# Query and recurrence products of a vision tower as sums of f16 halves, on one core

## Chip, core and metric

One core of a Trainium2 chip runs the whole program. The metric is the device time of one execution in microseconds (us); the time of the kernel before is the median of three. Engines are named as in the profile: PE is TensorE (PEld its weight loads), DVE is VectorE, ACT is ScalarE, POOL is GpSimd, SP is SyncE, which only issues DMAs.

## The reference, cut to what matters

```python
x = features.reshape(b, c, h, s, w, s)                 # 32 x 256 x 16 x 4 x 16 x 4
reduce_feats = x.mean((3, 5)).reshape(b, c, hw).transpose(0, 2, 1)
q = _ln(reduce_feats, ln_q_w, ln_q_b) @ Wq.T           # the queries
kv = _ln(unf, ln_kv_w, ln_kv_b) @ Wkv.T
attn = softmax(einsum('bhpd,bhpnd->bhpn', q * scale, k)); aggre = einsum('bhpn,bhpnd->bhpd', attn, v)
h = reduce_feats + aggre @ proj_w.T + proj_b           # then a class token in front of each image
...
xp = einsum('tbi,hi->tbh', layernorm(h), W_ih) + b_ih + b_hh
h_new = tanh(xp_t + h @ W_hh.T)                        # scan over the 32 images, 257 tokens wide
h = h + hiddens
h = h + moe(layernorm(h))                              # 8 experts, the best 2 of each token
```

All of it is f32; the recurrence runs over the images, one step per image for all its tokens.

## The kernel before, in words

The program has two stages. Stage A makes tokens, attention, recurrence and routing; stage B is the experts. Only stage A is touched. It works in 64 units of 128 tokens (two units an image), one slot per unit, and a slot carries four units at different depths: `u` (front) is loaded, averaged and given its queries; `v = u-1` (mid) gets scores and softmax; `w = u-2` (back) gets values and output projection; `z = u-3` (end) gets its step of the recurrence; `u-4` (late) is routed. Each engine has a function `slot` whose calls stand in a fixed order, written by hand; engines meet only at semaphores (`wait(engine, semaphore, ...)`). An engine carries out its queue in order, so a wait holds up all that stands behind it.

The steps that matter, in the order of a slot:

- PE `means` (L876) averages the pixels; ACT `mean_out` brings the mean from the bank FB to `rT`; DVE `mean_stats` and `mean_norm` make the norm `rn`; PE `turn_rn` (L884) transposes it into FB; ACT `rn_out` (L725) copies it to `rnT`; PE `queries` (L892) multiplies it with `wq_s` into FB; ACT `q_out` adds the bias and writes `qT`; PE `project` (L904) goes on with it.
- DVE `unmask` (L1151) cuts the scores `sm` out of the bank SB, PE `fold_patches` (L935) sums them, DVE `logits_in`, `total`, `divide` (up to `pr`, L1175) with ACT `exps` between make the softmax, PE `turn_p` (L942) transposes it.
- For the recurrence DVE `token_norm` (L1206) makes `xn`, PE `turn_xn` (L993) transposes it into the bank RB, ACT `xn_out` copies it to `xnT`, PE `recur` (L1005 with `hh_s` and the old `hT`, L1007 with `ih_s` and `xnT`) makes the new state, ACT `hidden` applies tanh into `hT`, PE `turn_h` turns it back, DVE `token_out` adds it to the tokens.
- POOL makes the inverse roots; of them `rs_wide` is what `turn_rs` (L912), the last PE step of a slot, waits for. SP reloads the buffers `xc` and `xp` as steps free them.

In some slots DVE also does a piece of the routing at the end of its list (`route_piece`: six steps or so in most of the eight pieces of a group of tiles). Ahead of the slots stands a prologue that scales the weights: DVE makes `wq_s` (L1267), then `rn` of unit 0, then `wk_s` (from L1270); the last link before the slots on PE is the class token's `xnT` (ACT L858).

Of the kernel before, what the change touches and what calls it, by code (L numbers as in the profile page):

```python
# [5 lines left out]
P = 128  # L6
# [10 lines left out]
CC = C // P  # L17
# [99 lines left out]
def vit_tower(nc, xc_in, xp_in, cls_tok, ln_q_w, ln_q_b, wqT, ln_kv_w, ln_kv_w_col, ln_kv_b, wk, wvT, projT, proj_b,  # L117
# [6 lines left out]
    with ctx:  # L124
# [50 lines left out]
        def sa(name, shape, dt=F32):  # L175
# [11 lines left out]
        wq_s = sa("wq_s", [P, CC, C])  # L187
# [3 lines left out]
        ih_s = sa("ih_s", [P, CC, C])  # L191
        hh_s = sa("hh_s", [P, CC, C])
# [10 lines left out]
        rnT = sa("rnT", [P, CC, P])  # L203
# [25 lines left out]
        xnT = sa("xnT", [P, CC, P + 1])  # L229
        hT = [sa(f"hT{i}", [P, CC, P + 1]) for i in range(2)]  # L230
# [9 lines left out]
            rT_ps rT_done q_stat q_var q_ve_done q_rs_done rn_done rc_done rn_ps rnT_done q_ps qT_done u_ps u_done  # L240
            st_done px_ve_done px_done wide_done own_done rep_ps rep_done s_ps s_masked c_ps sc_done c_max c_sub ex_done
            p_sum p_rec p_done pt_ps pd_done z_ps z_done zt_ps zT_done a_ps aT_done pj_ps h_done h_stat h_var h_ve_done h_rs_done
            xn_done nt_ps xnT_done h_ps hT_done ht_ps h2_done clsH_done
# [21 lines left out]
        stage_b = xc[1][:, :, :].rearrange("p c (h n) -> p (c h) n", n=C)  # L265
        projb_row = stage_b[:, 0, :]
# [270 lines left out]
        def _(sp):  # L537
            row_of = lambda a, n: a.partition_broadcast(n)
            for dst, src in ((spread[:, :], spread_in), (ident[:, :], ident_in)):
# [5 lines left out]
                     (ih_s[:, :, :], wihT.rearrange("(c p) n -> p c n", p=P)),  # L545
                     (hh_s[:, :, :], whhT.rearrange("(c p) n -> p c n", p=P)),
# [9 lines left out]
            sp.wait_ge(s["w_ready"], 2)  # L556
            load_xc(sp, 1, 1)
# [65 lines left out]
        def _(pool):  # L623
# [4 lines left out]
            for i in range(2):  # L628
                pool.memset(hT[i][:, :, :], 0.0).then_inc(s["mem_set"], 1)
            pool.memset(ones[:, :], 1.0).then_inc(s["mem_set"], 1)  # L630
            pool.wait_ge(s["mem_set"], 5)
# [33 lines left out]
            def keep_cls(pool, z):  # L665

                wait(pool, s["hT_done"], z, 2, 2)
                b = z.j * HALVES + z.k // HALVES
                pool.tensor_copy(clsH[:, :, bass.ds(b, 1)], hT[0][:, :, P:P + 1]).then_inc(s["clsH_done"], 1)
# [31 lines left out]
        def _(act):  # L701
# [20 lines left out]
            def rn_out(act, u):  # L722

                wait(act, s["rn_ps"], u, 1, 1)
                act.activation(rnT[:, :, :].rearrange("p c t -> p (c t)"), FB[:, 0:C], ACT.Copy).then_inc(s["rnT_done"], 1)  # L725

            def q_out(act, u):

                wait(act, s["q_ps"], u, 1, 1)
                for m in range(CC):  # L730
                    act.activation(qT[:, m, :], FB[:, m * P:(m + 1) * P], ACT.Identity, bias=qb_col[:, m:m + 1]).then_inc(s["qT_done"], 1)
# [41 lines left out]
            def xn_out(act, z):  # L773

                wait(act, s["nt_ps"], z, 1, 1)
                wait(act, s["h_ps"], z, 1, 0)
                act.activation(xnT[:, :, 0:P], RB[:, 0:C].rearrange("p (c t) -> p c t", t=P), ACT.Copy).then_inc(s["xnT_done"], 1)

            def hidden(act, z):

                wait(act, s["h_ps"], z, 1, 1)
                n = P + 1 if z.two == 0 else P
                if z.two == 0 and z.k > 0:
                    act.wait_ge(s["clsH_done"], z.k // HALVES)
                for m in range(CC):
                    act.activation(hT[z.two][:, m, 0:n], RB[:, m * 256:m * 256 + n], ACT.Tanh,
                                   bias=rnn_b[:, m:m + 1]).then_inc(s["hT_done"], 1)
# [13 lines left out]
            def slot(act, u, front, mid, back, end, late):  # L801
# [26 lines left out]
                if late:  # L828
                    route_logits(act, u.k - 4, FB)
                if mid:  # L830
                    z_out(act, v, [0, 1])
# [25 lines left out]
            act.wait_ge(s["mem_set"], 5)  # L857
            act.activation(xnT[:, :, P:P + 1], FB[:, 0:CC * B].rearrange("p (c b) -> p c b", b=B)[:, :, 0:1],  # L858
                           ACT.Copy).then_inc(s["w_ready"], 1)
            act.wait_ge(s["prep_act"], 4)  # L860
# [3 lines left out]
        def _(pe):  # L864
# [22 lines left out]
            def queries(pe, u):  # L887

                wait(pe, s["rnT_done"], u, 1, 1)
                for m in range(CC):  # L890
                    for c in range(CC):
                        last = mm(FB[:, m * P:(m + 1) * P], wq_s[:, c, m * P:(m + 1) * P], rnT[:, c, :],  # L892
                                  start=(c == 0), stop=(c == CC - 1))
                last.then_inc(s["q_ps"], 1)
# [101 lines left out]
            def recur(pe, z, m):  # L996

                n = P + 1 if z.two == 0 else P
                o = RB[:, m * 256:m * 256 + n]
                w = slice(m * P, (m + 1) * P)  # L1000
                if m == 0:
                    wait(pe, s["xnT_done"], z, 1, 1)
                    wait(pe, s["hT_done"], z, 2, -2)
                for c in range(CC):
                    mm(o, hh_s[:, c, w], hT[z.two][:, c, 0:n], start=(c == 0), stop=False)  # L1005
                for c in range(CC):
                    last = mm(o, ih_s[:, c, w], xnT[:, c, 0:n], start=False, stop=(c == CC - 1))  # L1007
                if m == CC - 1:
                    last.then_inc(s["h_ps"], 1)

            def turn_h(pe, z):

                wait(pe, s["hT_done"], z, 2, 2)
                for c in range(CC):
                    last = pe.transpose(RB[:, c * P:(c + 1) * P], hT[z.two][:, c, 0:P], ident[:, :])
                last.then_inc(s["ht_ps"], 1)

            def slot(pe, u, front, mid, back, end, late):
# [16 lines left out]
                if mid:  # L1035
                    fold_patches(pe, v)
                if end:
                    turn_xn(pe, z)
                if front:
                    queries(pe, u)  # L1040
# [42 lines left out]
            pe.wait_ge(s["prep_dve"], 4)  # L1083
            queries(pe, first)
            pe.wait_ge(s["mem_set"], 5)
# [3 lines left out]
            pe.wait_ge(s["prep_dve"], 8)  # L1089
# [3 lines left out]
            pe.wait_ge(s["prep_dve"], 10)  # L1093
# [8 lines left out]
            pe.wait_ge(s["w_ready"], 2)  # L1102
            pe.wait_ge(s["tri_done"], 1)
# [4 lines left out]
        def _(dve):  # L1108
# [33 lines left out]
            def mean_norm(dve, u):  # L1142
# [3 lines left out]
                dve.tensor_scalar(rn[:, :], rT[:, :], qmv[:, 0:1], q_rs[:, 0:1], ALU.subtract, ALU.mult).then_inc(s["rn_done"], 1)  # L1146

# [60 lines left out]

            def token_out(dve, z):
# [14 lines left out]
            def slot(dve, u, front, mid, back, end, late):  # L1224
# [8 lines left out]
                if mid:  # L1233
                    unmask(dve, v)
                if end:
                    token_norm(dve, z)
# [8 lines left out]
                if mid:  # L1245
                    total(dve, v)
                    divide(dve, v)
                if front:
# [6 lines left out]
                if end:  # L1255
                    token_out(dve, z)
                for g, part in pieces_now(u.k):
# [35 lines left out]
            dve.tensor_tensor(cvec[:, :], RB[:, 0:C], projb_row, ALU.add).then_inc(s["w_ready"], 1)  # L1293
            over_slots(dve, slot)
# [359 lines left out]
```

## Time and profile before

| | |
|---|---|
| median of 3 runs | 1449.83 us (1447.99 to 1450.88) |
| the profiled execution | 1449.13 us, its span 1447.3 us |
| PE busy | 1312.8 us (91%) |
| DVE busy | 1029.4 us (71%) |
| ACT busy | 816.7 us (56%) |
| POOL busy | 713.2 us (49%) |
| mean granted TensorE clock | 0.974 |
| DMA, mean | 293 GB/s |

Busy time is a mean over both stages. Stage A runs from the start to about 1100 us, its slots begin at 31 us; stage B fills the rest. An f32 product appears as two records on PE (and two weight loads), so `queries`, four products in the code, are eight records; an f16 product is one.

### The profile page before, as it was taken

Reading aid. Unit: us, or ns where it says so; the run is one execution under the profiler, and the core shown is the slowest. Engines: PE = TensorE matmul, PEld = TensorE weight load, DVE = VectorE, ACT = ScalarE, POOL = GpSimd, SP = SyncE. Lnnn points to the kernel's source line nnn. Section 1 sums busy time; section 2 is a strip of 40 time slices with the busy share of each in tenths; the row PEclk is TensorE's granted clock in tenths of the full one; section 3 lists DMA queues with packets and bytes.
Section 4 is the critical chain, followed back from the end, with each engine's and each line's share of the span. In section 5 each row is a group of like instructions: output and inputs, shape, how many; then the busy total and the mean of one; then the engine's idle time right before and its main releaser. Section 6 shows DMA issues by size and latency. Waiting matters only on the chain. (4 is left out here: it accounts for less than half of the span.)

```text
span 1447.3 us, 61906 instructions
## 1 busy us (share of the span) xinstructions
PE 1312.8 (91%) x25169; PEld 1071.8 (74%) x25169; DVE 1029.4 (71%) x2724; ACT 816.7 (56%) x1999; POOL 713.2 (49%) x852
## 2 busy tenths in 40 slices
PE   5799999999999999999999999999986999899960
PEld 3577788778777787777777777777865999777850
DVE  4677777777767777787876676778764686588874
ACT  1466556555656556555555555556555777555630
POOL 1344344434443434343466666664421577776476
PEclk8999999999999999999999999999998999999995
DMA  8999889999999999988899999998543788799897
GB/s 270 406 320 320 294 299 309 314 299 303 303 296 307 301 302 314 303 288 275 295 335 323 334 342 344 336 333 301 187 131 112 229 293 292 251 316 337 284 289 220
DMA packets 186614, 423.70 MB, mean 293 GB/s; under 512 B 23968, under 2 KB 89312, under 8 KB 186208
## 3 DMA queue, kind: packets, MB, share of 16 engines
q1 hardware_dynamic: 170336, 380.27, 77.3%
q0 software_dynamic: 14048, 38.16, 8.2%
q8 instruction: 205, 3.36, 0.9%
q10 hardware_dynamic: 1952, 1.32, 0.3%
q14 instruction: 73, 0.60, 0.1%
HBM read 332.26 MB, written 87.39 MB: 290 GB/s over the span
## 5 line engine op out<-in xcount | busy, mean ns | idle before, releaser
L1123 DVE BATCH_NORM_STATS2 st<-xp 128x6 f32<-128x512 f32 x512 | 340.3, 696 | 15.7 <-DMA xp<-xpix 15.2
L651 POOL TENSOR_TENSOR rs_px<-px_ve,half_neg 128x16 f32<-128x16 f32 x64 | 187.0, 2922 | 175.6 <-DVE px_ve L1128 175.6
L765 ACT ACTIVATE zT<-bank 128x512 f32<-128x512 f32 x256 | 138.6, 597 | 82.1 <-PE bank L966 82.1
L758 ACT ACTIVATE z_s<-bank 128x512 f32<-128x512 f32 x256 | 138.7, 597 | 80.7 <-PE bank L956 80.7
L925 PE MATMUL bank<-xc,u 128*32 128x64 f32 x8192 | 147.3, 220 | 25.1 <-issue 24.4
L925 PEld LDWEIGHTS bank<-xc,u 128*32 128x32 f32 x8192 | 130.1, 110 | 51.2 <-issue 40.3
L739 ACT ACTIVATE u<-bank 128x512 f32<-128x512 f32 x256 | 132.2, 602 | 49.1 <-PE bank L904 49.1
L1420 POOL DMA_INDIRECT y<-ys_dram,slot x130 | 129.3, 995 | 59.0 <-issue 36.3
L636 POOL TENSOR_TENSOR q_rs<-q_ve,half_neg 128x1 f32<-128x1 f32 x64 | 35.1, 549 | 244.5 <-DVE q_ve L1140 244.5
L966 PE MATMUL bank<-ident,z_s 128*128 128x128 f32 x1024 | 150.7, 280 | 2.2 <-issue 1.4
L412 POOL DMA_INDIRECT xs_dram<-xrow,slot x130 | 130.8, 1006 | 39.5 <-issue 34.6
L876 PE MATMUL bank<-xp,spread 128*32 128x256 f32 x2048 | 126.8, 389 | 14.5 <-DMA xp<-xpix 13.3
L956 PE MATMUL bank<-xp,pd 64*32 64x256 f32 x4096 | 126.7, 382 | 3.2 <-ACT u L739 3.2
L1457 ACT ACTIVATE g<-bank,b_s 128x256 f32<-128x256 f32 x172 | 82.0, 477 | 75.8 <-PE bank L1507 54.2
L966 PEld LDWEIGHTS bank<-ident,z_s 128*128 128x128 f32 x1024 | 112.0, 141 | 14.5 <-issue 1.6
L1192 DVE TENSOR_TENSOR h_s<-bank,rc 128x256 f32<-128x256 f32 x64 | 27.2, 425 | 125.1 <-PE bank L985 125.1
L1520 PE MATMUL bank<-xp,gh 128*128 x344 | 94.2, 274 | 14.3 <-DVE gl L1554 14.0
L876 PEld LDWEIGHTS bank<-xp,spread 128*32 128x32 f32 x2048 | 61.6, 111 | 56.4 <-issue 17.6
L1570 DVE SCALAR_TENSOR_TENSOR y_s<-bank,b_rep 128x512 f32<-128x512 f32 x86 | 59.4, 690 | 58.2 <-PE bank L1522 40.7
L956 PEld LDWEIGHTS bank<-xp,pd 64*32 64x32 f32 x4096 | 74.6, 107 | 34.7 <-issue 11.6
L1135 DVE BATCH_NORM_STATS2 qst<-rT 128x6 f32<-128x256 f32 x64 | 27.3, 426 | 96.0 <-ACT rT L720 95.9
L1505 PE MATMUL bank<-xT,xp 128*128 128x256 f16 x344 | 94.7, 275 | 0.3 <-ACT gh L1457 0.3
(178 smaller groups left out, 3142.6 us busy)
## 6 DMA issues: line engine op xcount, KB each, us to landing
xp<-xpix SPq DMA_DIRECT2D x256, 512.0 KB
xc<-xg SPq DMA_DIRECT2D x256, 512.0 KB
xc<-xs_dram SPq DMA_DIRECT2D x86, 256.0 KB
ys_dram<-y_s SPq DMA_DIRECT2D x86, 256.0 KB
xs_dram<-zero SPq DMA_DIRECT2D x57, 384.0 KB, 5.6
base_dram<-h SPq DMA_DIRECT2D x65, 128.0 KB, 5.7
rows_dram<-tok SPq DMA_DIRECT2D x65, 128.0 KB
hb<-base_dram SPq DMA_DIRECT2D x65, 128.0 KB, 4.3
```

The costliest lines, as they stand in the source:

```text
L412: pool.indirect_dma_start(xs_dram[g], bass.IndirectOffsetOnAxis(ap=slot_u[k][0:n, t:t + 1], axis=0), xrow[i][0:n, :], None).then_inc(sent[ ...
L651: pool.tensor_tensor(rs_px[:, :], px_ve[:, :], half_neg[:, :], ALU.pow).then_inc(s["px_done"], 1)
L739: act.activation(uv[:, k, :, :, :], BIG[k][:, :].rearrange("p (m a t) -> p m a t", m=CC, t=TS), ACT.Copy).then_inc(s["u_done"], 1)
L758: act.activation(z_s[:, r, 2 * half:2 * half + 2, :].rearrange("p a c -> p (a c)"), BIG[2 * r + half][:, :], ACT.Copy).then_inc(s["z_done" ...
L765: act.activation(zT[:, c, :, :].rearrange("p h (a r t) -> p r h a t", r=2, t=TS)[:, r, :, :, :], BIG[f][:, :].rearrange("p (a h t) -> p h ...
L876: last = mm(FB[32 * k:32 * k + 32, 0:C], spread[:, 24 - 8 * q:56 - 8 * q], xp[u.x][:, 4 * k + q, :], start=(q == 0), stop=(q == 3))
L925: last = mm(SB[32 * k:32 * k + 32, (2 * n + r) * SUB:(2 * n + r + 1) * SUB], u_s[u.two][:, c, g, :, :].rearrange("p h t -> p (h t)"), xc[u ...
L956: last = mm(BIG[2 * r + half][32 * k:32 * k + 32, n * C:(n + 1) * C], pd[64 * r:64 * r + 64, g, :, :].rearrange("p h t -> p (h t)"), xp[v. ...
L966: last = pe.transpose(BIG[f][:, n * P:(n + 1) * P], z_s[:, r, n, c * P:(c + 1) * P], ident[:, :])
L1123: dve.bn_stats(st[:, j, :], xp[u.x][:, 2 * j:2 * j + 2, :].rearrange("p i c -> p c i")).then_inc(s["st_done"], 1)
L1420: pool.indirect_dma_start(y[q][0:n, :], None, ys_dram[g], bass.IndirectOffsetOnAxis(ap=slot_u[k][0:n, t:t + 1], axis=0)).then_inc(ga_in[q] ...
L1505: mm(o, wh, xh, start=(c == 0), stop=False)
```

## The change

The two products for the queries and the recurrence are no longer f32 products. Each f32 operand is split into an f16 high half and an f16 low half (the rest), and each product is three f16 products added up in the bank: high with high, low weight with high, high weight with low. So `queries` has 12 f16 products for 4 f32 ones, `recur` 24 for 8. Weights are scaled by 64 before they are split; ACT takes the factor out again (`scale=1.0 / WSC`).

High halves are written by ACT in the copies that were there (`rnT_h`, `xnT_h`), and for the state by a new copy `hidden_high` behind the routing logits. Low halves are three new DVE steps: `mean_low` behind `unmask`, `token_low` behind `divide`, `hidden_low` behind `token_out`. `queries` waits for `mean_low`, `recur` for `token_low` and for the `hidden_low` of the slot before. On PE `queries` now stands ahead of `turn_xn`. The state `hT` in f32 has one buffer for two.

In the prologue DVE splits the query weights (two steps over 128x512 before `rn`) and does `mean_low` for unit 0; ACT and DVE split the recurrence weights (two steps each) behind the class token's `xnT_h`, and PE and SP wait for that (`rec_w`) before the slots and before the loads of `xc` 1 and `xp` 2.

```diff
 def rn_out(act, u):
     wait(act, s["rn_ps"], u, 1, 1)
-    act.activation(rnT[...], FB[:, 0:C], ACT.Copy).then_inc(s["rnT_done"], 1)
+    wait(act, s["q_ps"], u, 1, 0)
+    wait(act, s["rnl_done"], u, 1, 0)
+    act.activation(rnT_h[...], FB[:, 0:C], ACT.Copy).then_inc(s["rnT_done"], 1)
...
+def hidden_high(act, z):
+    n = P + 1 if z.two == 0 else P
+    wait(act, s["hT_done"], z, 2, 2)
+    act.activation(hT_h[z.two][:, :, 0:n], hT[:, :, 0:n], ACT.Copy).then_inc(s["hh_done"], 1)
...
 def queries(pe, u):
     wait(pe, s["rnT_done"], u, 1, 1)
+    wait(pe, s["rnl_done"], u, 1, 1)
...
-            last = mm(FB[...], wq_s[...], rnT[:, c, :], ...)
+            mm(o, wq_h[:, c, w], rnT_h[:, c, :], start=(c == 0), stop=False)
+            mm(o, wq_l[:, c, w], rnT_h[:, c, :], start=False, stop=False)
+            last = mm(o, wq_h[:, c, w], rnT_l[:, c, :], start=False, stop=(c == CC - 1))
...
 def recur(pe, z, m):
         wait(pe, s["xnT_done"], z, 1, 1)
-        wait(pe, s["hT_done"], z, 2, -2)
+        wait(pe, s["xnl_done"], z, 1, 1)
+        wait(pe, s["hl_done"], z, 1, -1)
...
+def mean_low(dve, u):
+    wait(dve, s["rnT_done"], u, 1, 1)
+    wait(dve, s["q_ps"], u, 1, 0)
+    dve.tensor_tensor(rnT_l[:, :, :], FB[...], rnT_h[:, :, :], ALU.subtract).then_inc(s["rnl_done"], 1)
...
+def token_low(dve, z):
+    wait(dve, s["xnT_done"], z, 1, 1)
+    dve.tensor_tensor(xnT_l[:, :, 0:P], RB[...], xnT_h[:, :, 0:P], ALU.subtract).then_inc(s["xnl_done"], 1)
+
+def hidden_low(dve, z):
+    wait(dve, s["hh_done"], z, 1, 1)
+    dve.tensor_tensor(hT_l[z.two][:, :, 0:n], hT[:, :, 0:n], hT_h[z.two][:, :, 0:n], ALU.subtract)...
...
+dve.wait_ge(s["prep_pe"], 1)
-    chain(dve.tensor_scalar(wq_s[:, c, :], raw_q[:, c, :], lq_w[:, c:c + 1], None, ALU.mult))
+    chain(dve.tensor_scalar(raw_q[:, c, :], raw_q[:, c, :], lq_w[:, c:c + 1], None, ALU.mult))
+chain(dve.tensor_scalar(wq_h[:, :, :], raw_q, WSC, None, ALU.mult))
+chain(dve.scalar_tensor_tensor(wq_l[:, :, :], raw_q, WSC, wq_h[:, :, :], ALU.mult, ALU.subtract))
 mean_norm(dve, first)
+mean_low(dve, first)
...
+for raw, high in ((raw_ih, ih_h), (raw_hh, hh_h)):
+    act.activation(high[:, :, :], raw, ACT.Copy, scale=WSC).then_inc(s["rec_hi"], 1)
...
+dve.wait_ge(s["rec_hi"], 2)
+for raw, high, low in ((raw_ih, ih_h, ih_l), (raw_hh, hh_h, hh_l)):
+    dve.scalar_tensor_tensor(low[:, :, :], raw, WSC, high[:, :, :], ALU.mult, ALU.subtract)...
```

On PE, in the middle of a full slot, this is the order before, from the last turn of `z_s` to `values` (`ident,xn` is `turn_xn`, `rnT,wq_s` are the queries):

```order
L966 MATMUL bank<-ident,z_s 128x128 x4
L935 MATMUL bank<-sm,pick 32x128 x4
L993 MATMUL bank<-ident,xn 128x128 x2
L892 MATMUL bank<-rnT,wq_s 128x128 x4
L977 MATMUL bank<-zT,wv_s 32x128 x16
```

And this is the same place of the change; the three products of the queries come four times.

```order
L989 MATMUL bank<-ident,z_s 128x128 x4
L958 MATMUL bank<-sm,pick 32x128 x4
L914 MATMUL bank<-rnT_h,wq_h 128x128
L915 MATMUL bank<-rnT_h,wq_l 128x128
L916 MATMUL bank<-rnT_l,wq_h 128x128
...
L1016 MATMUL bank<-ident,xn 128x128 x2
L1000 MATMUL bank<-zT,wv_s 32x128 x16
```

The turn of `xn` has moved from ahead of the queries to behind them, so nothing stands between `fold_patches` and the queries.

On DVE, from `unmask` to `pd` of a full slot, the order before is:

```order
L1151 TENSOR_TENSOR sm<-bank,fold 128x512
L1206 TENSOR_SCALAR xn<-h_s,hmv,h_rs 128x256
L313 TENSOR_SCALAR tok<-h_1,emv,ers 128x256
L1123 BN_STATS st<-xp 128x6
...
L1173 RECIPROCAL rden<-den 128x8
L1175 TENSOR_TENSOR pr<-ex,rden 128x128
L1123 BN_STATS st<-xp 128x6
L1128 TENSOR_SCALAR px_ve<-st 128x16
L1183 TENSOR_TENSOR pd<-bank,rs_own 128x512
```

In the change two steps have come in, `rnT_l` (`mean_low`) and `xnT_l` (`token_low`):

```order
L1187 TENSOR_TENSOR sm<-bank,fold 128x512
L1181 TENSOR_TENSOR rnT_l<-bank,rnT_h 128x256
L1242 TENSOR_SCALAR xn<-h_s,hmv,h_rs 128x256
L316 TENSOR_SCALAR tok<-h_1,emv,ers 128x256
L1152 BN_STATS st<-xp 128x6
...
L1209 RECIPROCAL rden<-den 128x8
L1211 TENSOR_TENSOR pr<-ex,rden 128x128
L1248 TENSOR_TENSOR xnT_l<-bank,xnT_h 128x2x128
L1152 BN_STATS st<-xp 128x6
L1157 TENSOR_SCALAR px_ve<-st 128x16
L1219 TENSOR_TENSOR pd<-bank,rs_own 128x512
```

Everything from `xn` to `pr` now stands behind one new step, and what follows `pr` behind two.

## Rows read from the trace of the kernel before

**Rows 1.** By stretch: busy us of PE, PEld, DVE, ACT, POOL; clock; DMA share; GB/s.

```profile
200.00:300.00 100.00, 98.42 (x2205) 79.64 (x2202) 74.31 (x215) 59.79 (x152) 40.92 (x52) 1.00 0.91 306
```

**Rows 2.** Timeline, PE in one slot: start us, us, engine, line, records [idle before].

```profile
224.91 0.33 PE L912 MATMUL bank<-ident,rs_wide 128*128 128x128 f32 x1
...
231.43 0.43 PE L935 MATMUL bank<-sm,pick 128*32 128x128 f32 x8
...
231.78 0.44 PE L993 MATMUL bank<-ident,xn 128*128 128x128 f32 x2
...
232.06 1.06 PE L892 MATMUL bank<-rnT,wq_s 128*128 128x128 f32 x8
...
235.54 0.61 PE L1005 MATMUL bank<-hT,hh_s 128*128 128x129 f32 x4
...
237.33 1.03 PE L985 MATMUL bank<-pj_s,aT 128*128 128x256 f32 x4
...
240.79 0.33 PE L912 MATMUL bank<-ident,rs_wide 128*128 128x128 f32 x1
```

**Rows 3.** Timeline, the same slot on DVE, ACT and POOL.

```profile
227.66 0.43 DVE L1135 BATCH_NORM_STATS2 qst<-rT 128x6 f32<-128x256 f32 x1 [1.67 <-ACT rT L720]
...
230.69 0.68 DVE L1151 TENSOR_TENSOR sm<-bank,fold 128x512 f32<-128x512 f32 x1
...
230.90 0.39 ACT L725 ACTIVATE rnT<-bank 128x256 f32<-128x256 f32 x1 [1.19 <-PE bank L884]
...
231.29 0.41 DVE L1206 TENSOR_SCALAR xn<-h_s,hmv,h_rs 128x256 f32<-128x256 f32 x1
...
234.57 0.29 DVE L1175 TENSOR_TENSOR pr<-ex,rden 128x128 f32<-128x128 f32 x1
...
238.76 0.41 POOL L654 TENSOR_TENSOR rs_wide<-rs_px,ones 128x128 f32<-128x128 f32 x1
```

**Rows 4.** Timeline, f16 products of the routing ranks, PE, then PEld.

```profile
660.76 0.37 PE L440 MATMUL bank<-oh,ones 128*128 128x128 f16 x4
...
660.81 0.39 PE L440 MATMUL bank<-oh,ones 128*128 128x120 f16 x5
...
660.87 0.15 PEld L440 LDWEIGHTS bank<-oh,ones 128*128 128x128 f16 x2
```

**Rows 5.** Groups by line on DVE: busy us, mean ns | idle before, releasers.

```profile
L1559 DVE TENSOR_TENSOR xT<-bank,xT 128x512 f16<-128x512 f32 x86 | 58.8, 684 | 3.5 <-ACT xT L1442 3.4
...
L1192 DVE TENSOR_TENSOR h_s<-bank,rc 128x256 f32<-128x256 f32 x64 | 27.2, 425 | 125.1 <-PE bank L985 125.1
```

**Rows 6.** Waits of the whole span: us in total, times, longest.

```profile
PE bank L925 <- issue: 24.4, 27, 2.1
```

**Rows 7.** Timeline of one slot with such a stall.

```profile
424.98 0.41 DVE L1206 TENSOR_SCALAR xn<-h_s,hmv,h_rs 128x256 f32<-128x256 f32 x1
425.14 0.38 ACT L725 ACTIVATE rnT<-bank 128x256 f32<-128x256 f32 x1 [1.19 <-PE bank L884]
...
428.05 0.29 DVE L1168 TENSOR_REDUCE den<-ex 128x8 f32<-128x128 f32 x1 [0.28 <-ACT ex L751]
```

**Rows 8.** Timeline, PE in a slot behind a routing piece.

```profile
618.88 0.42 PE L935 MATMUL bank<-sm,pick 128*32 128x128 f32 x8 [0.47 <-DVE sm L1151]
```

**Rows 9.** Timeline of the prologue.

```profile
18.82 0.35 DVE L1267 TENSOR_SCALAR wq_s<-xc,lq_w 128x256 f32<-128x256 f32 x1 [0.59 <-DMA pj_s<-projT]
18.84 1.05 PE L1074 MATMUL bank<-lq_b,xc 128*128 128x1 f32 x8 [1.92 <-DMA pj_s<-projT]
...
20.70 0.68 DVE L1270 TENSOR_TENSOR xc<-xc 128x512 f32<-128x512 f32 x1
...
21.62 0.38 ACT L725 ACTIVATE rnT<-bank 128x256 f32<-128x256 f32 x1 [0.29 <-PE bank L884]
...
31.32 3.24 PE L876 MATMUL bank<-xp,spread 128*32 128x256 f32 x32 [0.31 <-ACT xnT L858]
```

**Rows 10.** Groups by line, an f16 copy on ACT: columns as in Rows 5.

```profile
L799 ACT ACTIVATE xp<-xc 128x512 f16<-128x512 f32 x16 | 8.7, 632 | 2.1 <-DMA xc<-w 2.1
```

More of the change, by code:

```diff
@@ L186, in vit_tower @@
         qb_col = sa("qb_col", [P, CC])
-        wq_s = sa("wq_s", [P, CC, C])
+        wq_h, wq_l = [sa(f"wq_{n}", [P, CC, C], F16) for n in "hl"]
         wk_s = sa("wk_s", [P, CC, C])
@@ L190, in vit_tower @@
         pj_s = sa("pj_s", [P, CC, C])
-        ih_s = sa("ih_s", [P, CC, C])
-        hh_s = sa("hh_s", [P, CC, C])
+        ih_h, ih_l = [sa(f"ih_{n}", [P, CC, C], F16) for n in "hl"]
+        hh_h, hh_l = [sa(f"hh_{n}", [P, CC, C], F16) for n in "hl"]
         cvec = sa("cvec", [P, C])
@@ L202, in vit_tower @@
         rn = sa("rn", [P, C])
-        rnT = sa("rnT", [P, CC, P])
+        rnT_h, rnT_l = [sa(f"rnT_{n}", [P, CC, P], F16) for n in "hl"]
         qT = sa("qT", [P, CC, P])
@@ L228, in vit_tower @@
         xn = sa("xn", [P, C])
-        xnT = sa("xnT", [P, CC, P + 1])
-        hT = [sa(f"hT{i}", [P, CC, P + 1]) for i in range(2)]
+        xnT_h, xnT_l = [sa(f"xnT_{n}", [P, CC, P + 1], F16) for n in "hl"]
+        hT = sa("hT", [P, CC, P + 1])
+        hT_h = [sa(f"hT_h{i}", [P, CC, P + 1], F16) for i in range(2)]
+        hT_l = [sa(f"hT_l{i}", [P, CC, P + 1], F16) for i in range(2)]
         zero = sa("zero", [P, C])
@@ L556, in _ @@
             sp.wait_ge(s["w_ready"], 2)
+            sp.wait_ge(s["rec_w"], 3)
             load_xc(sp, 1, 1)
@@ L829, in slot @@
                     route_logits(act, u.k - 4, FB)
+                if end:
+                    hidden_high(act, z)
                 if mid:
@@ L1036, in slot @@
                     fold_patches(pe, v)
+                if front:
+                    queries(pe, u)
                 if end:
                     turn_xn(pe, z)
-                if front:
-                    queries(pe, u)
                 if back:
@@ L1102, in _ @@
             pe.wait_ge(s["w_ready"], 2)
+            pe.wait_ge(s["rec_w"], 3)
             pe.wait_ge(s["tri_done"], 1)
@@ L1207, in token_norm @@
                                   ALU.mult).then_inc(s["xn_done"], 1)
+            def token_low(dve, z):
+                wait(dve, s["xnT_done"], z, 1, 1)
+                dve.tensor_tensor(xnT_l[:, :, 0:P], RB[:, 0:C].rearrange("p (c t) -> p c t", t=P), xnT_h[:, :, 0:P],
+                                  ALU.subtract).then_inc(s["xnl_done"], 1)
+            def hidden_low(dve, z):
+                n = P + 1 if z.two == 0 else P
+                wait(dve, s["hh_done"], z, 1, 1)
+                dve.tensor_tensor(hT_l[z.two][:, :, 0:n], hT[:, :, 0:n], hT_h[z.two][:, :, 0:n],
+                                  ALU.subtract).then_inc(s["hl_done"], 1)
             def token_out(dve, z):
@@ L1234, in slot @@
                     unmask(dve, v)
+                if front:
+                    mean_low(dve, u)
                 if end:
@@ L1247, in slot @@
                     divide(dve, v)
+                if end:
+                    token_low(dve, z)
                 if front:
@@ L1256, in slot @@
                     token_out(dve, z)
+                    hidden_low(dve, z)
                 for g, part in pieces_now(u.k):
@@ L1293, in _ @@
             dve.tensor_tensor(cvec[:, :], RB[:, 0:C], projb_row, ALU.add).then_inc(s["w_ready"], 1)
+            dve.wait_ge(s["rec_hi"], 2)
+            for raw, high, low in ((raw_ih, ih_h, ih_l), (raw_hh, hh_h, hh_l)):
+                dve.scalar_tensor_tensor(low[:, :, :], raw, WSC, high[:, :, :], ALU.mult, ALU.subtract).then_inc(s["rec_w"], 1)
+            dve.wait_ge(s["w_ready"], 2)
+            dve.tensor_tensor(xnT_l[:, :, P:P + 1], FB[:, 0:CC * B].rearrange("p (c b) -> p c b", b=B)[:, :, 0:1],
+                              xnT_h[:, :, P:P + 1], ALU.subtract).then_inc(s["rec_w"], 1)
             over_slots(dve, slot)
```

60 lines of the change are left out of this document (35 added, 25 removed).

## The prediction

> **What bounds the kernel now.** First the busy time by stretch: in a stretch from the middle of stage A, PE works 98.42 of 100 us at the full granted clock (1.00), the upper of its two levels, DVE 74.31, ACT 59.79, POOL 40.92 [rows 1]. So PE bounds the slots, and a slot is as long as PE's list. The timeline of one slot shows it: from one turn of `rs_wide` to the next 15.88 us (224.91 to 240.79) without an idle note on PE [rows 2]. The question is who is late next when PE's list gets shorter, and that is read from the same slot on DVE [rows 3]: it idles 1.67 us ahead of `qst`, and from there its steps follow each other without a gap to `pr`, which ends at 234.86, only 0.68 us before PE starts the recurrence at 235.54. The new steps go into just this chain. Not all slots look so: in 27 of 63 PE stands inside the scores (L925) for something that the profile doesn't show, 24.4 us in all [rows 6], and behind a routing piece it waits for DVE's `sm` (0.47 us in the one shown) [rows 8]; I put 8 slots down to that, somewhat fewer than the long pieces of two groups, since the second group's steps are shorter. That leaves 28 plain slots.
>
> **The products.** The recurrence's 16 f32 records take 237.33 - 235.54 = 1.79 us, 0.112 each [rows 2]. The trace has f16 products of 128 columns, each with a weight load: the one of 128 columns starts at 660.76, the next at 660.81, so 0.05 apart, and their two weight loads lie within 0.15 us, overlapping [rows 4]. Half an f32 record is 0.056; I take that. Recurrence: 24 x 0.056 = 1.34, a gain of 0.45 us. Queries: 8 x 0.112 = 0.90 to 12 x 0.056 = 0.67, a gain of 0.23. On PE's list alone that is 0.68 us a slot.
>
> **mean_low.** It subtracts f16 from a PSUM bank, 128x256. DVE's nearest row of that size is `h_s` with 0.425 us; half as wide is `pr` with 0.29, twice as wide and with f16 written is L1559 with 0.684 [rows 3, 5]. I take 0.42, between 0.29 and 0.68. It stands behind `unmask`, which leaves DVE free at 231.29, and needs `rnT`, which ACT ends at 231.29 [rows 3]: with 0.08 for the signal it runs from 231.37 to 231.79. PE takes a DVE result 0.06 us after its end (`sm` ends at 231.37, L935 starts at 231.43) [rows 2, 3], so the queries start at 231.85. `fold_patches` is done at 231.78 and `turn_xn` no longer fills the gap: PE waits 0.07 us. Turning `xn` behind the queries costs nothing, since `xn` is ready long before 232.5. Queued behind `mean_low` on DVE are `xn`, the routing norm, two statistics and the whole softmax. `xn` starts at 231.71 in place of 231.29, and `pr`, with no gap between to take it up, ends at 234.86 + 0.42 = 235.28.
>
> **token_low.** The same price. Steps overlap by 0.08 us (`xn` starts at 231.29, `sm` ends at 231.37), so it runs from 235.20 to 235.62, and the recurrence starts at 235.68, 0.14 later than before. The 0.23 us of the queries are thus lost in waits for DVE; with 1.34 us the recurrence ends at 237.02, 0.31 before the old 237.33. **A plain slot gains 0.31 us**, 28 of them 8.7. What else moves there has cover: `rs_wide` shifts by 0.42 + 0.34 to end at 239.93, while PE wants it at 240.48; without that cover each further tenth on DVE would cost a tenth.
>
> **hidden_high, hidden_low.** One ACT copy (at most 0.63, L799, which is twice as wide [rows 10]) and one DVE step (0.42). ACT is 60% busy [rows 1]; the DVE step lies in the 1.67 us ahead of `qst` [rows 3], and its result is wanted a slot later. Nothing; without DVE's cover, 0.34 us a slot, as behind the routing pieces.
>
> **Stalled slots.** Where PE stalls in the scores, `rnT` is late: in the slot shown it ends at 425.52, when DVE has been free since 424.98 [rows 7]. Before, DVE went on with `xn`; now it stands. `xn` starts at 425.94, 0.96 late. Some comes back, as `den` had waited 0.28 us there for the exponentials [rows 7], which now come no later than DVE's own steps allow: I take 0.6 at `pr`. In a plain slot 0.42 at `pr` became 0.14 at the recurrence, 0.28 less, so here the recurrence starts 0.6 - 0.28 = 0.32 later and a slot gains 0.45 - 0.32 = 0.13. Bounds: a gain of 0.31 if all is taken up, a loss of 0.2 if nothing is. 27 x 0.13 = 3.5.
>
> **Slots behind a routing piece.** There DVE is late already [rows 8], `hidden_low` adds its 0.34 and the recurrence moves by about what it gains: 0, between +0.2 and -0.3 each. Sum of the slots: 8.7 + 3.5 = 12.2 us.
>
> **The prologue** [rows 9, 10]. (a) The weights are now scaled in place, so DVE waits until PE has read them: 19.89 in place of 18.82, 1.1. (b) Two steps of 128x512 ahead of `rn`, 0.68 each: 1.4. (c) `mean_low` of unit 0 makes DVE wait for `rnT`: L1270 would start at 22.0 + 0.08 + 0.34 = 22.4, not 20.70: 1.7. From L1270 a chain of DVE, POOL and PE leads to `xnT`, on which PE waits until 31.32, so all 4.2 us arrive there. (d) Behind it come two ACT copies (0.63 and 0.52 with their overlap), two DVE steps (0.69 and 0.61) and a tiny one, less the 0.3 that PE's wait took before: about 2.5, which `rec_w` puts ahead of PE's first slot and of SP's loads behind it (`xc` 1 to `xp` 3, which move with the slot that needs them). 6.7 us, once; between 5 and 8, as (c) or (d) may hide a little. No later slack gives it back while slots follow each other on PE.
>
> **Sum.** 12.2 - 6.7 = 5.5 us. The profiled execution took 1449.13 us, 0.7 under the median of the runs and inside their spread: 1443.6 from the one, 1444.3 from the other. Forecast **1444**.
>
> **A rule against the change.** On pace, the row says 0.05 us from one f16 product of 128 columns to the next with loads in between [rows 4], though all these loads bring the same tile. The Trainium skill, "TensorE: Matmul & The Clock Gate", section "Back-to-back issue gap", says that a sustained stream of weight load and matmul goes at about 81 ns for 128 columns. By that the recurrence would take 24 x 0.081 = 1.94 us, longer than now, and the time an estimated 1472 us. The trace doesn't agree; the sum goes by the row.
>
> **The rivals.** *PE's gain arrives whole*: DVE takes the low halves up somewhere (cheap subtractions, near 0.29, and `rnT` earlier). Against it stands DVE's chain without a gap. 55 x 0.68 - 6.7 gives 1418. Chance 0.08.
> *DVE's chain gets longer than priced* (slower): the low halves write and read f16 beside a bank, and a row of that kind is L1559 with 0.684 us [rows 5]. At that price the recurrence starts 0.14 + 0.52 later and a slot loses 0.21: 55 x 0.21 + 6.7 gives 1467. It decides from 6.7 / 55 = 0.12 us gain per slot, that is once the two steps together come 0.19 us later than I put them; halfway it gives 1455. For it: nothing on DVE is slack there, and `rnT` is just in time. Chance 0.21.
> *The f16 products are paced by their weight loads*, 0.10 us each alone [rows 4], since here every product has weights of its own, so the change doesn't do what it says: 24 x 0.10 = 2.4, 0.75 more a slot, 1497. Against it: the overlap in the rows. Chance 0.05.
> *The prologue hides* behind loads that the slots wait for: 1439. Chance 0.05. My forecast has 0.61, its own range is 1437 to 1451.
>
> **How the numbers follow.** A measurement of this kernel tells 0.2%, 2.9 us, from no change. Of the forecast's 0.61, 0.45 lies below 1446.9, 0.13 within, 0.03 above; of the slower rival 0.05 lies within. Faster 0.45 + 0.08 + 0.05 = 0.58, same 0.18, slower 0.24. The range leaves out the whole gain, the weight loads and the far end of the slower rival: 1434 to 1458.
>
> **What the profile after would show.** Plain slots of 15.57 us; the f16 records 0.056 apart; on PE waits for `rnT_l` (under 0.1 us) and for `xnT_l` ahead of the recurrence (about 0.2) in plain slots; DVE idle ahead of `rnT_l` in stalled ones; the first slot starting near 38 us. Wrong, if plain slots are near 15.2 (no chain on DVE), above 15.76 (the low halves cost more), or if the records lie 0.08 or more apart.

## The result and the profile after

The change makes the kernel slower: 1487.82 us median (1485.09 to 1490.09) beside 1450.36 of before, a ratio of 1.0224 with a 95% interval of 1.0179 to 1.0269; that it is slower is clear, whether by 2% is not. The forecast was 1444.0 with a range up to 1458. The profiled execution took 1490.09 us, 0.15% over the median.

First a plain slot, one in which PE idles nowhere. The timeline of PE in after answers to [rows 2], with the two new DVE steps beside it; it goes from one turn of `rs_wide` to the next, and in the columns are start, length, line, tiles and count:

```profile
207.38 0.33 PE L935 MATMUL bank<-ident,rs_wide 128*128 128x128 f32 x1
...
213.78 0.42 DVE L1181 TENSOR_TENSOR rnT_l<-bank,rnT_h 128x256 f16<-128x256 f32 x1
214.35 0.22 PE L914 MATMUL bank<-rnT_h,wq_h 128*128 128x128 f16 x1
214.40 0.22 PE L915 MATMUL bank<-rnT_h,wq_l 128*128 128x128 f16 x1
...
215.02 0.39 PE L1016 MATMUL bank<-ident,xn 128*128 128x128 f32 x2
...
217.58 0.42 DVE L1248 TENSOR_TENSOR xnT_l<-bank,xnT_h 128x256 f16<-128x256 f32 x1
...
218.10 0.22 PE L1029 MATMUL bank<-hT_h,hh_h 128*128 128x129 f16 x1
218.16 0.22 PE L1030 MATMUL bank<-hT_l,hh_h 128*128 128x129 f16 x1
...
219.47 1.08 PE L1008 MATMUL bank<-pj_s,aT 128*128 128x256 f32 x4
...
222.99 0.33 PE L935 MATMUL bank<-ident,rs_wide 128*128 128x128 f32 x1
```

The slot takes 15.61 us (the ten plain ones 15.58 to 15.85, their median 15.60). The twelve products of the queries take 0.67 us (214.35 to 215.02), the 24 of the recurrence 1.37. So the plain slot came out nearly as forecast (15.57). But few slots are plain. What PE waits for, by line, in after (total us, times, longest), which answers to [rows 6]:

```profile
PE bank L948 <- issue: 36.6, 37, 2.2
...
PE bank L914 <- DVE rnT_l L1181: 9.7, 38, 1.0
...
PE bank L896 <- issue: 5.0, 2, 2.9
PE bank L1033 <- issue: 4.1, 3, 1.8
PE bank L935 <- POOL rs_wide L659: 3.6, 1, 3.6
PE bank L989 <- issue: 3.3, 5, 1.4
```

"Issue" is time in which PE waits for nothing that the profile shows. Before it was 24.4 us at one line and 3 us at others; now it is 36.6 us there and 26 at others. Summed over the 63 slots of stage A, from the first turn of `rs_wide` to the last, that is 61.7 us against 26.6. These slots lengthened from a mean of 16.48 to 17.05 us, 36.0 us in all: 35.1 of this are such waits, and the slots less these waits take 0.9 us more than before. The two profiled executions differ by 41.1 us; 3.2 of them lie ahead of the first slot and 1.9 behind the last. The granted clock in the stretch 200 to 300 us is 1.00 in both kernels, so it is no cause there:

```profile
core 0: us, PE busy (x) PEld busy (x) DVE busy (x) ACT busy (x) POOL busy (x), PEclk, DMA share, GB/s
200.00:300.00 100.00, 95.31 (x2220) 73.99 (x2215) 77.89 (x226) 60.42 (x152) 40.98 (x51) 1.00 0.90 298
```

PE's busy time fell from 98.42 [rows 1] to 95.31 of 100 us, and the last columns say that the DMA engines are 0.90 busy there.

One of the waits at L896 is no stall of the kind that follows. It is the start of the first slot, where PE waits for the recurrence weights (`rec_w`), whose last step DVE ends at 37.82:

```profile
37.66 0.16 DVE L1356 TENSOR_TENSOR xnT_l<-bank,xnT_h 128x2 f16<-128x2 f32 x1
...
38.03 3.64 PE L896 MATMUL bank<-xp,spread 128*32 128x256 f32 x32 [2.85 <-issue]
```

This belongs to the prologue. Without it the stalls are 58.9 us against 26.6.

**What the stalls are.** One of them stands inside the recurrence, between two products with no wait between them in the code. PE's timeline there:

```profile
416.00 0.22 PE L1031 MATMUL bank<-hT_h,hh_l 128*128 128x129 f16 x1
417.88 0.22 PE L1033 MATMUL bank<-xnT_h,ih_h 128*128 128x129 f16 x1 [1.66 <-issue]
417.94 0.22 PE L1034 MATMUL bank<-xnT_h,ih_l 128*128 128x129 f16 x1
```

I numbered PE's instructions in the two programs (an f32 product is two weight loads and two matmuls, an f16 product or a transpose one of each, an extra instruction that only waits one). All 29 stalls in the slots of before and all 58 in those of after (the 2.85 us aside) stand at the same place modulo 256 (193 to 196). The traces have 52,488 instructions of PE before and 54,089 after, which is 205.0 and 211.3 times 256, and the page of each kernel lists as many packets, of 16 KB each, on an instruction queue. The first row is before, the second after:

```profile
q8 instruction: 205, 3.36, 0.9%
```
```profile
q8 instruction: 211, 3.46, 0.9%
```

So PE's code comes by DMA, a block of 256 instructions at a time, and PE stands at a block's end until the next is there. For the stall above the DMA queues in the 0.4 us from 415.4 to 415.8 read (packets, MB, share of 16 engines):

```profile
q1 hardware_dynamic: 77, 0.11, 84.3%
q8 instruction: 1, 0.02, 14.8%
```

14.8% of 16 x 0.4 us is one packet of 0.95 us; it begins there, and PE goes on at 417.88. Over all stalls PE goes on 1.4 us after the end of such a packet, the middle half of them in a stretch of 0.11 us before and 0.16 after. The Trainium skill, "Runtime: NRT & Kernel Launch", section "Instruction fetch mechanics", says that code is fetched in blocks of 16 KiB or 256 instructions while the block before runs, and that the cost is mostly hidden. The trace agrees on the blocks; hidden it is not in stage A of these kernels, with 26.6 us of stalls before and 58.9 after.

**What a long stall costs besides.** In three slots of after behind the first two the granted clock falls at the end of a stall of 2.2 to 2.4 us; before has one such slot, with a stall of 2.1. One of the three (the third row is of the same view as the stretch above):

```profile
584.58 0.22 PE L1035 MATMUL bank<-xnT_l,ih_h 128*128 128x129 f16 x1 [2.38 <-issue]
...
586.06 2.02 PE L1008 MATMUL bank<-pj_s,aT 128*128 128x256 f32 x4
```
```profile
584.80:588.20 3.40, 3.40 (x22) 3.04 (x19) 0.08 (x1) 0.63 (x2) 1.15 (x3) 0.51 0.61 210
```

The clock is 0.51 there, the lower of its two levels, and the four records of L1008 take 2.02 us for the 1.08 of the plain slot. With 2.85 us of stalls the slot takes 20.5 us.

### The profile page after: what moved, and what is told of

Read it like the earlier page. It is cut to its first block and busy times, and to the rows that moved or that the text cites. A ratio compares the mean times of both kernels' runs of the same rounds, so it can differ in the third digit from the quotient of the medians.

```text
span 1488.4 us, 63932 instructions
## 1 busy us (share of the span) xinstructions
PE 1306.8 (88%) x25937; PEld 1039.9 (70%) x25937; DVE 1094.0 (74%) x2921; ACT 841.5 (57%) x2065; POOL 720.4 (48%) x854
## 5 line engine op out<-in xcount | busy, mean ns | idle before, releaser
L948 PE MATMUL bank<-xc,u 128*32 128x64 f32 x8192 | 152.4, 221 | 37.2 <-issue 36.6
L948 PEld LDWEIGHTS bank<-xc,u 128*32 128x32 f32 x8192 | 134.1, 111 | 64.2 <-issue 54.3
L1484 POOL DMA_INDIRECT y<-ys_dram,slot x130 | 129.8, 998 | 60.2 <-issue 36.6
L989 PE MATMUL bank<-ident,z_s 128*128 128x128 f32 x1024 | 152.2, 282 | 4.2 <-issue 3.3
L896 PE MATMUL bank<-xp,spread 128*32 128x256 f32 x2048 | 129.5, 392 | 18.6 <-DMA xp<-xpix 12.7
L641 POOL TENSOR_TENSOR q_rs<-q_ve,half_neg 128x1 f32<-128x1 f32 x64 | 35.1, 548 | 221.2 <-DVE q_ve L1169 221.2
L989 PEld LDWEIGHTS bank<-ident,z_s 128*128 128x128 f32 x1024 | 113.2, 142 | 17.1 <-issue 4.3
L896 PEld LDWEIGHTS bank<-xp,spread 128*32 128x32 f32 x2048 | 63.2, 112 | 61.1 <-issue 23.6
L333 POOL TENSOR_TENSOR h<-h,tok 128x256 f32<-128x256 f32 x65 | 47.3, 728 | 115.2 <-DVE tok L316 115.2
```

Of the source, the lines that this page charges most:

```text
L896: last = mm(FB[32 * k:32 * k + 32, 0:C], spread[:, 24 - 8 * q:56 - 8 * q], xp[u.x][:, 4 * k + q, :], start=(q == 0), stop=(q == 3))
L948: last = mm(SB[32 * k:32 * k + 32, (2 * n + r) * SUB:(2 * n + r + 1) * SUB], u_s[u.two][:, c, g, :, :].rearrange("p h t -> p (h t)"), xc[u ...
L989: last = pe.transpose(BIG[f][:, n * P:(n + 1) * P], z_s[:, r, n, c * P:(c + 1) * P], ident[:, :])
L1484: pool.indirect_dma_start(y[q][0:n, :], None, ys_dram[g], bass.IndirectOffsetOnAxis(ap=slot_u[k][0:n, t:t + 1], axis=0)).then_inc(ga_in[q] ...
```

## The experiments

A slot of PE has 717 instructions before and 742 after, since three f16 products are six instructions where an f32 product is four. My first theory was that the code's loads set stage A outright (5.88 us for 256 instructions in both kernels, stalls included). The rival was DVE: the low steps and the late `rnT_l`.

**e1_dve_only: the DVE half of the change.** Before, with

```diff
+                if front:
+                    mean_low(dve, u)
...
+                    token_low(dve, z)
...
+                    hidden_low(dve, z)
```

> Before with the three DVE steps, hidden_high and the new order of the queries, but with f32 products; the low halves are made and waited for, and read by nothing. PE's program is 2 instructions a slot longer than before. The code theory (a slot of stage A lasts as long as the loads of PE's code take: 717 instructions a slot before and 742 after, 5.86 us per 256 in both) gives 718/256 x 5.86 = 16.44 us a slot, about as before, plus 1.7 us of mean_low in the prologue: 1450 to 1462, with some 30 stalls of PE without a releaser in the trace. The DVE theory (the low steps and the late rnT_l make the 36 us) gives 1486 or more, since PE's list is longer by 0.68 us a slot than in after and all of DVE's steps are there.

Measured: 1481.75 us (1.0186 of before, 1.0116 to 1.0256). The first theory falls in this form: nearly the same code as before, and 28 us more; the rival, with 1486 or more, is missed by 4 us. In its profiled execution the slots are 36 us longer than in that of before. Of this plain slots of 16.05 us make 0.17 x 63 = 11, PE's waits for `rnT_l` in the slots with a stall 7.4, waits behind routing pieces some 4, and the stalls, 38 us against 27, make 12. Three slots at a granted clock of 0.92, behind long stalls, are in the rest.

**e2_pe_only: the PE half.** After without the low steps:

```diff
-                        last = mm(o, wq_h[:, c, w], rnT_l[:, c, :], ...)
+                        last = mm(o, wq_h[:, c, w], rnT_h[:, c, :], ...)
```

> After with its f16 products but without the three low steps on DVE: the third product reads the high half in place of the low one, so that half is left out of the result. PE's program has 742 instructions a slot as in after. The code theory gives 742/256 x 5.86 = 17.0 us a slot, so after less the 1.7 us of mean_low in the prologue: 1475 to 1490, with some 60 stalls. The DVE theory gives PE's whole gain: near 1418.

Measured: 1458.35 (1.0039, 1.0004 to 1.0073). Neither theory had it. Plain slots take 15.29 us, 0.59 less than before, which is 37 us; and the waits without a releaser take 65.4 us, of which 2.9 are the wait for `rec_w` and 62.5 are stalls, 36 more than before. PE's gain arrives, and nearly all of it is lost again in waiting for code:

```profile
PE bank L945 <- issue: 46.5, 42, 3.1
...
PE bank L893 <- issue: 5.5, 5, 2.9
PE bank L986 <- issue: 4.7, 5, 1.4
```

(its scores, means and turns of `z_s`; they answer to L948, L896 and L989 of after).

**e3_pad25 and e7_two_padded: more instructions, no more work.**

```diff
+                for _ in range(16):
+                    pe.wait_ge(s["tri_done"], 1)
```

(16 again behind the projection and 18 behind the recurrence; the program holds two such waits in one instruction, so these 50 waits are 25 instructions a slot.)

> Before with 25 more instructions a slot on PE, waits that have long been met, behind the values, the projection and the recurrence: 742 instructions a slot, no more work for the array, nothing new on DVE. The code theory gives 25/256 x 5.86 = 0.57 us a slot, 63 x 0.57 = 36 us: 1470 to 1490, with 50 to 65 stalls. The DVE theory, and any other on operands or products, gives 1450; were the waits themselves to take PE's time, plain slots without a stall would be longer than 15.88 us by what they take.

Measured: 1488.76 (1.0243, 1.0190 to 1.0297). The time is the one forecast, the reason isn't: plain slots take 16.24 us, so the added instructions themselves cost 14 ns each, 22 us in all, and the stalls at block ends are some 31 us, hardly more than before.

> After without the product of the low weight halves (left out of the result); each of these 12 products is replaced by two instructions that only wait for something long met, so PE has 742 instructions a slot as in after, but 12 x 0.056 = 0.67 us a slot less to do for the array. The code theory gives no change against after: 1480 to 1492. A theory by which PE's array work or DVE's steps bound the slots gives up to 0.67 us a slot less: 1446 to 1465.

Measured: 1508.3 (1.0388, 1.0316 to 1.0459), outside both ranges, and its plain slots take 16.21 us, where the same products without the filling take 15.15 (e6, next): 44 ns for each of the 24 instructions that only wait, between f16 products that otherwise follow each other in 56. So met waits are no neutral filling, and the two runs don't settle what the number of instructions does.

**e6_two_products: fewer instructions and less work.**

```diff
-                        mm(o, wq_l[:, c, w], rnT_h[:, c, :], start=False, stop=False)
...
-                    mm(o, hh_l[:, c, w], hT_h[z.two][:, c, 0:n], start=False, stop=False)
```

(and so for `ih_l`).

> After without the product of the low weight halves (left out of the result): 718 instructions a slot, as few as before, and 12 x 0.056 = 0.67 us a slot less for the array. Two readings of the stalls: if the number of instructions makes them, they fall back to the 27 us of before: 1487.8 - 42 - 34, that is 1410 to 1425. If it is how long a page of 256 instructions lasts (before 15.88 / 2.80 = 5.67 us, after 15.58 / 2.90 = 5.37, here 14.95 / 2.80 = 5.33), they stay near 60 us: 1440 to 1455.

Measured: 1481.7 (1.0212, 1.0161 to 1.0263), above both: 42 us less work for the array brought 6. With about as many instructions as before the stalls are the longest of the table, 72.5 us, so the number of instructions alone does not make them. How long a block of 256 lasts in a plain slot (the median of these slots) orders the kernels better:

| kernel | plain slot, us | instructions | us for 256 | stalls, us |
|---|---|---|---|---|
| e2_pe_only | 15.29 | 742 | 5.28 | 63 |
| after | 15.60 | 742 | 5.38 | 59 |
| e6_two_products | 15.15 | 718 | 5.40 | 73 |
| e7_two_padded | 16.21 | 742 | 5.59 | 38 |
| e3_pad25 | 16.24 | 742 | 5.60 | 31 |
| before | 15.89 | 717 | 5.67 | 27 |
| e8_before_fewer_waits | 15.88 | 711 | 5.72 | 23 |
| e1_dve_only | 16.05 | 718 | 5.72 | 38 |

(each from one profiled execution; those of one kernel differ by up to 1%). The three whose blocks are shortest stall for 59 to 73 us, the others for 23 to 38. The length of the slot alone, below 15.7 us or above, parts them in the same way, so the table doesn't tell a short block from the same loads in a shorter slot.

**e4_after_fewer_loads, e5_before_fewer_loads: why the code is late.**

```diff
                     load_xp(sp, w.x, w.k + XBUF, [0])
...
-                    load_xp(sp, w.x, w.k + XBUF, [1])
...
-                    load_xc(sp, v.c, v.k + XC, [1])
```

(and so for parts 2 and 3).

> After with one of the four part loads by which each slot refills xc and xp (the other three quarters keep old pixels, so they are left out of the result); PE's program and work unchanged. If PE's stalls are code loads that come late behind the pixel loads, they go (61.7 us in the slots of after), and with them the waits for rnT_l behind them (8.7): 1410 to 1428, plain slots still 15.57 us. If code is as slow to come without the pixel loads, or the stalls have another cause on PE, the time stays at 1480 to 1490.

> The same for the kernel before: one of four part loads of xc and xp. If the stalls are code loads behind the pixel loads, 27 us of stalls go: 1418 to 1428. Then after with fewer loads should be faster than this one by what the prediction gave for plain slots, some 5 to 10 us, since only the stalls had turned the sum. If the stalls have another cause: 1450.

Measured: 1423.37, inside the theory's range, and 1428.8, 0.8 us above it; the range of the other causes is far off. PE's waits without a releaser in the slots of stage A went from 61.7 to 8.9 us and from 26.6 to 9.9 (without the wait for `rec_w` 58.9 to 6.1 in after). In after with fewer loads, the stretch of 200 to 300 us and PE's waits in the scores and for `rnT_l` read:

```profile
200.00:300.00 100.00, 97.15 (x2324) 75.82 (x2316) 81.17 (x237) 62.34 (x158) 43.02 (x54) 1.00 0.36 109
```
```profile
PE bank L942 <- issue: 6.4, 8, 1.2
...
PE bank L908 <- DVE rnT_l L1175: 3.8, 12, 1.0
```

The DMA share is 0.36 for 0.90, the program on PE is the same, and plain slots keep their length (15.60 and 15.88), so the loads don't slow the array itself. So the stalls are code that waits behind pixel loads. From PE's crossing of one block's end until it has the code that it needs at the next end, a mean of 4.7 us passes before and 5.2 after, and 3.5 and 3.7 with fewer loads (from the packets' times in the traces); the packet's own length hardly moves (median 0.96 us in all four), its start does: 2.2 and 2.8 us behind the crossing, and 1.0 and 1.3 with fewer loads. No slot behind the first two shows a lower clock there. And with most stalls gone, after is faster than before, by 5.4 us.

**e14_dve_only_fewer_loads, e15_pe_only_fewer_loads: each half without the stalls** (the edits of e1 and e2 with that of e4).

> The kernel with the DVE steps and the order alone (f32 products), with one of four part loads of xc and xp (old pixels in the rest, left out of the result). Its slots without a stall took 16.05 us against 15.88 of before, 0.17 more, and it has mean_low in the prologue (1.7) and some 4 us behind the routing pieces. Without most of the stalls that gives 1428.8 + 63 x 0.17 + 1.7 + 4 = 1445, between 1440 and 1450. If the DVE steps cost what the run with all loads showed (28 us), stalls or not: 1455 to 1460.

> The f16 products without the low steps (high half twice, the low half is left out of the result), with one of four part loads. Slots without a stall took 15.29 us with all loads, 0.59 less than before. If only the late code had taken this gain back: 1428.8 - 63 x 0.59 + 2.5 (prologue) = 1394, between 1388 and 1402. If f16 products have a cost of their own that the plain slots don't show: 1415 to 1428.

Measured: 1445.26 and 1398.97, both as the terms of the sum have it. Against 1428.8 the products alone gain 29.8 us and the DVE steps alone cost 16.5; together that would be 1415.5, and after has 1423.4. The 8 us between show in the plain slots: 15.60 us, where 15.88 + 0.17 - 0.59 would be 15.46. That f16 queries leave less to hide `mean_low` behind would explain it, but no run shows that.

**e10_old_order: the norm of the recurrence ahead again.**

```diff
                 if end:
+                    turn_xn(pe, z)
+                if front:
+                    queries(pe, u)
-                if front:
-                    queries(pe, u)
-                if end:
-                    turn_xn(pe, z)
```

(and `token_norm` ahead of `mean_low` on DVE).

> After with the old order at one place: DVE makes xn ahead of mean_low, and PE turns xn ahead of the queries, as in before. In after's stalled slots PE waits 0.23 us for rnT_l (37 slots) and a slot less its stall takes 15.98 us, no less than the 15.95 of before. If that is DVE standing idle for a late rnT with xn queued behind, the old order gives 0.2 to 0.3 us back in some 45 slots and may cost up to 0.1 in the others: 1474 to 1482. If the order doesn't matter: 1485 to 1490. If the low halves' own length is the cost, the same 1485 to 1490.

Measured: 1490.75 (1.0270, 1.0211 to 1.0328), no gain. The trace has both halves of the answer: the wait for `rnT_l` is gone and a slot with a stall, less that stall, takes 15.74 us for 15.97 (medians); but the waits without a releaser are 71 us for 62. What PE gets back it gives to the code again.

**e12, e13, e16, e17: the same loads at other times.** Each part load of `xc` one step of PE earlier (e12 before, e13 after):

```diff
+                    wait(sp, s["rn_ps"], u, 1, 1)
+                    load_xc(sp, v.c, v.k + XC, [0])
                     wait(sp, s["q_ps"], u, 1, 1)
-                    load_xc(sp, v.c, v.k + XC, [0])
+                    load_xc(sp, v.c, v.k + XC, [1])
```

> The same move of the xc loads in the kernel before: 1428 to 1447 beside its 1450 if the stalls in the scores are code that waits behind the bunch of loads at the end of a slot; 1447 to 1453 if only the total counts.

> After with the four part loads of xc each issued one step of PE earlier (behind the turned rn, the queries, the values and the projection in place of the queries, the values, the projection and the output projection); the same bytes, the same program on PE. In the trace of after the DMA engines are 0.8 to 0.87 busy from 1 to 9 us into a plain slot and 0.95 to 1.0 from 11 us to its end, where the code for the next scores is asked for. If the stalls are code that waits behind this bunch of pixel loads, they get fewer: 1450 to 1478. If only the total of the loads counts, not their time: 1483 to 1492. If the earlier loads meet other code pages: slower than 1492.

Measured: 1458.89 (1.0059, 1.0027 to 1.0091) and 1502.14 (1.0365, 1.0323 to 1.0408); e12 lies above both its ranges, e13 in its third. One step later (e16 before, e17 with the edit of e8 too):

> Before with each part load of xc one step of PE later (values, projection, output projection, first half of the weighing), the opposite of the move that cost 0.6%. If what counts is how late the loads sit in front of the code of the long pages (queries to output projection): 1440 to 1448 beside 1450 of before. If the order of before is the best and any move makes bunches: 1453 to 1462.

> The same later loads in the kernel without the implied waits on PE (711 instructions a slot): 5 us below the run with the later loads alone, as without them (1447 beside 1453), so 1435 to 1443, or 1448 to 1457 if the move costs.

Measured: 1467.8 (1.0119, 1.0059 to 1.0179) and 1462.91 (1.0087, 1.0055 to 1.0118), above all the ranges. Stalls of 40 us (e12) and 37 us (e16) for the 27 of before, with plain slots unchanged at 15.88 to 15.89; in e16 six slots run at a granted clock of 0.91 or 0.92, for one in before. My picture of a bunch of loads at a slot's end falls, as both directions lose; that the time of the loads matters, apart from their sum, is shown, though it is little: 0.6 and 1.2% in before (e12, e16), and in after 1.0365 for 1.0224 (e13). Which load meets which block stays open.

**e8_before_fewer_waits: six instructions fewer a slot.**

```diff
-                wait(pe, s["h2_done"], z, 1, 0)
...
-                wait(pe, s["h_done"], w, 1, 0)
```

(and five more waits a slot that an earlier wait of PE implies).

> Before without waits on PE that an earlier wait of PE implies: 711 instructions a slot in place of 717, the same work. The padded kernel had 14 ns for each such instruction in a plain slot (16.23 against 15.88 us for 25). So plain slots of 15.80 us, 5 us in all; and pages of code that last as long as before in time, so stalls of 24 to 30 us: 1442 to 1447 beside 1450 of before. If PE's instruction count alone sets stage A (5.86 us per 256): 6/256 x 5.86 x 63 = 8.7 us, 1441. If neither: 1450.

Measured: 1447.17 beside 1453.35 of before on the same chip (0.9954, 0.9923 to 0.9985). Its plain slots stay at 15.88, not the 15.80 expected, so the waits cost nothing there; the stalls are 23 us. The gain is outside the noise by the interval, but only 0.5%. e17 lies 5 us under e16, but their intervals overlap, and the waits without a releaser are the same (37.6 and 37.3 us), so it is not shown a second time.

## Why the prediction was wrong

**The step that failed** is the one that put the stalls down as a constant: "in 27 of 63 PE stands inside the scores (L925) for something that the profile doesn't show, 24.4 us in all" [rows 6]. It was read, left unexplained and carried into the sum unchanged. It was the term with the largest change: 26.6 to 58.9 us. In the forecast's terms, the profiled executions give: 6.1 us for the prologue (6.7 forecast), 32.3 more of stalls (0 forecast), 0.9 more for the slots less their stalls (12.2 less forecast) and 1.9 behind the slots. The 12.2 went with it, as 45 slots stall and not 27, and a stalled slot gains nothing (below). The fewer loads of e4 and e5 take the stalls away in both kernels, and the change gains. The rows to see it were there: a wait without a releaser, at the same instruction modulo 256 each time, an instruction queue in the DMA table, and a change that adds 25 instructions a slot and shortens the slot. None of the three signs that the prediction gave for being wrong came (plain slots near 15.2 us, above 15.76, records 0.08 apart): they all looked at plain slots.

**The products**: right. 0.056 us apart (0.67 and 1.37 us for forecast 0.67 and 1.34). The rival of pacing by weight loads falls with them. The 81 ns of the Trainium skill ("TensorE: Matmul & The Clock Gate", "Back-to-back issue gap") falls too: the trace doesn't agree with that figure for these products, at 56 to 57 ns each.

**mean_low and token_low**: right. They take 0.42 us each, as forecast; `mean_low` starts 0.04 us behind the end of `rnT_h`, where 0.08 were taken. In the slot shown the recurrence starts 0.10 us behind the end of `token_low` (218.00 to 218.10) and 10.72 us into the slot, for 10.63 before [rows 2]: 0.09 later, where 0.14 were forecast. Plain slots have a median of 15.60 for 15.57. Without the DVE steps it is 15.29 (e2), so the DVE steps take 0.31 of the 0.59 that PE's list gains; I had 0.37 of 0.68. The rival of dearer low halves falls.

**Plain slots**: their price was right, their number wrong, 17 slots without a stall for the 28 plus 8 assumed.

**Stalled slots**: forecast gain 0.13 each; measured, less the stall, a median of 15.97 us for 15.96 of before, no gain. The mechanism was right (DVE stands idle for `rnT_h` ahead of `rnT_l` 40 times, 22.2 us in all; PE waits 0.23 us for `rnT_l` in most of 37 slots), its size lay between what I took and the lower bound of -0.2. What the list lacks is the lower clock behind the longest stalls.

**Behind routing pieces**: right. With few stalls (e4 against e5) the 13 slots behind a piece, less their stalls, differ by 0.02 us in the mean: 0, as forecast. PE waits longer there for `sm` and `rn` (8.3 us in the slots for 4.1), about what its list got shorter.

**hidden_high, hidden_low**: nothing, as forecast; nothing in the traces waits for them in plain slots.

**The prologue**: right. PE turns `rs_wide` for the first slot at 32.64 for 29.40, behind a wait of 3.6 us, and starts the slot's `means` at 38.03, near the 38 forecast, for 31.32 [rows 9]: 6.71 us later, where 6.7 were forecast. The second slot starts 6.5 us later than before. It doesn't hide.

**The rivals**: that PE's gain arrives whole falls, as plain slots keep 0.28 of 0.59 us; e15 shows it nearly whole only without DVE's steps and most stalls. The slower side came out, but by none of the mechanisms listed, and past the range.

**A number that fits by luck.** The 5.4 us between e5 and e4 are not the forecast's 5.5 come true. That sum had 27 stalled slots at 0.13 us; with no stalls its own prices give 55 x 0.31 - 6.7 = 10.4. In the profiled executions of e5 and e4 the slots from the second on are 16.8 us shorter (55 x 0.31 = 17), 3.8 us of it by fewer stalls, and the second slot starts 11.0 us later, not 6.7.

What stays open: why e1 stalls for 12 us more than before with nearly the same code (executions of one kernel spread by up to 1%, so part of it may be that), and how much of the growth in after is from the 25 added instructions, how much from the shorter slot. e6 shows only that the number alone doesn't do it.

## What to carry to other kernels

A wait that the profile puts down to nothing is a term of the sum like any other: look where it sits, by the count of instructions on its engine, before it is carried over as a constant. Where an unrolled program runs beside loads that keep the DMA engines 0.9 busy, work taken from the bound engine is worth what the code's arrival allows: here (e2) 37 us of array time became 36 us of waiting. The signs by which a forecast would be wrong should look at the slots that stall, too. To split f32 products into three f16 ones is faster on the array and half as long again in instructions; try it first where the DMA engines are idle.

## What the runs showed of the hardware

PE's program comes in packets of 16 KB for 256 instructions. A packet takes 0.96 us itself, PE goes on 1.4 us after its end, and from one block end until PE had the code for the next one took 3.5 to 3.7 us in the mean with a DMA share near 0.36 (e5, e4), and 4.7 to 5.2 us with 0.9 (before, after). Where PE had worked off a block sooner than its successor was there, it stood.

An instruction that only waits, for something long met, cost 14 ns behind groups of f32 products (e3) and about 44 ns between f16 products (e7 against e6); the six taken out in e8 cost nothing in a plain slot.

Behind a stall of 2.38 us the granted clock of TensorE was 0.51 from 584.80 to 588.20, its lower level, and four records that take 1.08 us in a plain slot took 2.02 (after).
